# 23 instead of 24 tiles a group in a fused transformer-like kernel, seven steps of the recurrence beside each sorted unit, long operations moved between steps

## What is computed

```python
xn = layernorm(x)
x = x + linear_attention(xn) + moe0(xn)      # moe0: 16 experts of 176 units, top 6, softmax weights
xn = layernorm(x)
x = x + recurrence(xn) + moe1(xn)

def recurrence(x):                           # 512 numbers of state for each of the 4 sequences
    u = x @ W_in.T + b_in
    state = tanh(u[:, t] + state * gamma + beta)     # for t in 0 .. 511, one after the other
    return states @ W_out.T + b_out

def moe1(x):                                 # 8 experts of 176 units, top 2, and 2 shared experts
    topk_w, topk_idx = top_k(softmax(x @ gate.T), 2); topk_w /= topk_w.sum()
    y = sum over the 2 chosen e of topk_w * (silu(x @ wg[e].T) * (x @ wu[e].T)) @ wd[e].T
    return y + silu(x @ sg.T) * (x @ su.T) @ sd.T
```

## Time and profile before

| | us |
|---|---|
| median of 3 runs | 677.58 |
| lowest, highest | 676.92, 679.07 |
| the profiled execution | 680.39 |
| its span, first to last instruction | 678.80 |

### The profile page before, as it was taken

The page is one execution under the profiler, slowest core; times in us unless marked ns, Lnnn a source line. Parts: engine busy times, 40 slices in busy tenths (PEclk is TensorE's granted clock), DMA queues, the critical chain, the costliest instruction groups (busy, mean ns, idle before and its releaser), DMA issues. The chain is left out here.

```text
span 678.8 us, 12642 instructions
## 1 busy us (share of the span) xinstructions
PE 624.3 (92%) x3607; PEld 343.8 (51%) x3607; DVE 448.0 (66%) x1519; ACT 369.1 (54%) x1008; POOL 247.4 (36%) x267
## 2 busy tenths in 40 slices
PE   6999899999999988999999989999877899888985
PEld 2665344544444434444454434454554576656754
DVE  7873876567943767674677775567682756774666
ACT  2445445456446456567556666746456647563550
POOL 5246222222242125532225523223610342653483
PEclk8999999999999999999999999999987899988998
DMA  8103577773495435852556620507322455752133
GB/s 305 60 1 132 188 247 242 246 233 95 141 341 188 153 104 173 267 185 96 177 187 209 218 93 1 214 11 123 87 38 63 93 143 129 174 153 77 40 113 99
DMA packets 91228, 99.06 MB, mean 146 GB/s; under 512 B 30478, under 2 KB 81774, under 8 KB 90734
## 3 DMA queue, kind: packets, MB, share of 16 engines
q10 hardware_dynamic: 45840, 46.40, 20.9%
q1 hardware_dynamic: 39950, 37.21, 19.0%
q0 software_dynamic: 5376, 14.69, 7.2%
...
## 5 line engine op out<-in xcount | busy, mean ns | idle before, releaser
L1876 POOL TENSOR_TENSOR hl<-scr,hh 128x512 f16<-128x512 f32 (+2 forms) x100 | 115.9, 1159 | 288.7 <-ACT hh L1265 287.1
L1295 ACT ACTIVATE RING<-zbuf 128x16 f32<-128x16 f32 x512 | 111.0, 217 | 149.6 <-DVE zbuf L1732 145.3
L714 PE MATMUL G<-xT,W 128*128 128x512 f16 (+2 forms) x600 | 146.3, 380 | 4.9 <-ACT scr L1257 2.9
L714 PE MATMUL U<-xT,W 128*128 128x512 f16 (+2 forms) x600 | 147.2, 382 | 2.7 <-DVE scr L1747 2.7
L1732 DVE TENSOR_TENSOR_SCAN zbuf<-C,RING 128x32 f32<-128x32 f32 x350 | 77.0, 220 | 76.1 <-ACT RING L1295 75.7
L714 PE MATMUL Y<-hh,W 128*128 128x512 f16 x352 | 119.3, 380 | 6.7 <-POOL hl L1876 6.6
L714 PEld LDWEIGHTS U<-xT,W 128*128 128x128 f16 (+3 forms) x600 | 61.4, 103 | 72.4 <-DVE scr L1747 4.0
L714 PEld LDWEIGHTS G<-xT,W 128*128 128x128 f16 (+3 forms) x600 | 60.1, 102 | 69.7 <-issue 5.1
L1753 DVE TENSOR_TENSOR U<-U,CS 128x512 f32<-128x512 f32 x88 | 60.4, 686 | 39.2 <-PE U L714 32.7
L1257 ACT ACTIVATE scr<-G 128x512 f32<-128x512 f32 (+2 forms) x100 | 58.8, 588 | 47.1 <-PE G L714 46.6
L1265 ACT ACTIVATE hh<-scr 128x512 f16<-128x512 f32 (+2 forms) x100 | 61.8, 618 | 28.8 <-DVE scr L1747 26.1
...
...
## 6 DMA issues: line engine op xcount, KB each, us to landing
...
W<-parked SPq DMA_DIRECT2D x1, 3520.0 KB, 11.6
```

The source lines that it names most:

```text
L714: last = nc.tensor.matmul(bank_, w(wp), act(ap), start=start and n == 0, stop=stop and n == count - 1)
L1295: nc.scalar.activation(RING[:, (t + 1) % RING_T, ::2], zbuf[:, 1::2], ACT.Tanh).then_inc(state_done, 1)
L1876: nc.gpsimd.tensor_tensor(hl[rows, a, :], h32[a][rows, :], hh[rows, a, :], ALU.subtract)\
```

## The change

There are 23 tiles in a group. Two groups have 46 tiles, 23 tile units; the twelfth (pair 11) has the last tile of the first group and the first of the second. So there are 35 units: 0 to 2 shared, 3 to 25 tiles, 26 to 34 shared. A tile unit carries seven steps, a shared one six: 312 + 18 + 23 x 7 + 18 = 509 steps lie before unit 29, which has the last three. In a tile unit the seventh step follows step 5 on both engines. What was listed for units 26 and later stands one unit earlier, `hold_gamma` (a copy of gamma into PSUM for the scans of the last units) two.

A new table `UNIT_GAPS` names operations that are called behind step i of unit u instead of in front of a unit: the row copy of block 3, the exponential, the four input copies, and all heads and tails of the states of blocks 1 to 3. Those of block 1 move from the fronts of units 6 to 9 to units 1 to 4, those of block 2 from units 21 to 24 to units 20 to 23, those of block 3 from units 34 and 35 to units 30 to 33. The two turn buffers in PSUM (`HT`) change places.

```diff
+UNIT_STEPS = {"S": SLOTTED, "R": SLOTTED + 1}
-TILES = 24
+TILES = 23
...
-         + [("R", group, q) for group in (0, 1) for q in range(TILES // 2)]
+         + [("R", 2 * r // TILES, r) for r in range(len(GROUPS) * TILES // 2)]
...
-        HT = (G, C)
+        HT = (C, G)
...
-        UNITS_HELD = (0, 1, 2, 30, 31, 32, 33)
+        UNITS_HELD = (0, 1, 2, 28, 29)
...
-            5: [("shared_add", (0, Y[0])), ("norm_turn", (7, Y[1])), ("rows", (3, 0))],
-            6: [("logits", (7, Y[1][1])), ("rows", (3, 1)), ("split_states", (1, 0))],
-            7: [("inputs", (3, 0, Y[1])), ("exp", (7,)), ("split_states", (1, 1))],
-            8: [("inputs", (3, 2, Y[1])), ("split_states", (1, 2))],
-            9: [("rank", (3, Y[1][1])), ("split_states", (1, 3))],
-            10: [("scatter", (3, 0)), ("scatter", (3, 1))],
+            5: [("shared_add", (0, Y[0])), ("norm_turn", (7, Y[1]))],
+            6: [("logits", (7, Y[1][1]))],
+            7: [("inputs", (3, 0, Y[1]))],
+            8: [("inputs", (3, 2, Y[1]))],
+            9: [("rank", (3, Y[1][1]))],
+            10: [("more_inputs", (4,)), ("scatter", (3, 0)), ("scatter", (3, 1))],
...
-            21: [("split_states", (2, 0))],
-            22: [("split_states", (2, 1))],
-            23: [("split_states", (2, 2))],
-            24: [("split_states", (2, 3))],
-            26: [("attend", (2, Y[1]))],
-            30: [("hold_gamma", (BLOCKS,))],
-            32: [("shared_add", (1, Y[1]))],
-            34: [("split_states", (3, 0)), ("split_states", (3, 1))],
-            35: [("split_states", (3, 2)), ("split_states", (3, 3))],
+            25: [("attend", (2, Y[1]))],
+            28: [("hold_gamma", (BLOCKS,))],
+            31: [("shared_add", (1, Y[1]))],
...
+        UNIT_GAPS = {(5, 3): ("rows", (3, 0)), (5, 5): ("rows", (3, 1)),
+                     (7, 0): ("input_copy", (3, 0, Y[1][0])), (7, 2): ("input_copy", (3, 1, Y[1][1])), (6, 4): ("exp", (7,)),
+                     (8, 0): ("input_copy", (3, 2, Y[1][0])), (8, 2): ("input_copy", (3, 3, Y[1][1])),
+                     **{(1 + c, 3): ("states_head", (1, c)) for c in range(KH)},
+                     **{(1 + c, 5): ("states_tail", (1, c)) for c in range(KH)},
+                     **{(20 + c, 3): ("states_head", (2, c)) for c in range(KH)},
+                     **{(20 + c, 5): ("states_tail", (2, c)) for c in range(KH)},
+                     **{(30 + c, 2): ("states_head", (3, c)) for c in range(KH)},
+                     **{(30 + c, 4): ("states_tail", (3, c)) for c in range(KH)}}
...
+        def unit_gap(u, gap, share):
+
+            name, args = UNIT_GAPS.get((u, gap), (None, ()))
+            if name in share:
+                share[name](*args)
...
+        def steps_to(u):
+
+            return STEPS * TICKS0 + sum(UNIT_STEPS[UNITS[m][0]] for m in range(u))
+
+        def group_of_pair(r):
+
+            return (2 * r + 1) // TILES
...
             def unit_step(u, i):
-                step(TICKS0, SLOTTED * u + i)
+                state_at(steps_to(u) + i)
+                unit_gap(u, i, gaps)
...
-                unit_step(u, 5)
+                for i in range(5, UNIT_STEPS[kind(n)]):
+                    unit_step(u, i)
...
                 def unit_step(i):
-                    step(TICKS0, SLOTTED * u + i, u in UNITS_HELD)
-                    if u in UNIT_WOVEN:
+                    scan_at(steps_to(u) + i, u in UNITS_HELD)
+                    if u in UNIT_WOVEN and i < SLOTTED:
...
+                    unit_gap(u, i, {"states_tail": split_states})
```

78 lines of the change are left out of this document (44 added, 34 removed).

## The result

The changed kernel takes 673.53 us (median of 8 runs) beside 679.21 us for the kernel before (median of 8). The ratio is 0.992, 95% interval 0.9901 to 0.9939: faster by 5.4 us, give or take 1.3. The prediction was 672.0 us, 5.6 us saved. The profiled execution took 674.63 us with a span of 673.0 us; that of before 680.39 and 678.8. The forecast of 672.0 was counted from 677.58 us, the median of three runs; over eight the kernel before has 679.21. One of the eight runs of the changed kernel took 807.01 us at a granted clock of 0.75 and is left out of the ratio; the other seven took 671.8 to 675.9 us.

The account below looks back on a forecast made before the run. It took the scan-tanh chain on VectorE and ScalarE, held by operations between steps, as the bound where TensorE isn't full; -2.6 + 0 + 0.6 - 2.9 - 0.7 = -5.6 us off 677.58 gave 672.0 us, range 667 to 679.

Parts of the forecast that it names:

- Units 1 to 8: Units 1 to 8: 17.7 us of front stops removed, less seventh steps, gap operations and late input products; -2.6 us.
- The moves alone: Units 1 to 8: moving stages from fronts into gaps, without the 3.1 us for six seventh steps.
- Units 9 to 13: Units 9 to 13: seventh steps vanish in waits for the stores' DMA and the attention products; 0, bound +2.5 us.
- 14 to 18: Units 14 to 18: five units of 3.84 us, 19.2 us instead of 18.6; +0.6 us.
- rival (b): Units 9 to 18: the seventh step isn't absorbed, ten cost 5.1 us instead of 0.6; 676.5 us, no change; chance 0.20.
- Units 19 to 25: Units 19 to 26, afterwards 19 to 25: one tile unit goes and most of it is kept; -2.9 us.
- gap prices: Units 20 to 23: added to the 3.84 us chain, combines 0.6, head with silu 0.8, tail 0.6; 5.8 us each.
- the two units behind them: Two units behind units 20 to 23: 608.85 to 621.74 us as before; one seventh step hidden, the other costs 0.5 us.
- rival (a): Units 1 to 8 and 20 to 23: spread waits keep TensorE's clock low; 14.6 us in all, 682 at two thirds; chance 0.13.
- The shared units: Units 26 to 34: the recurrence ends in unit 29 instead of 33, freeing the last head before the gathers; -0.7 us.
- Behind the gathers: From the first of the last 16 GpSimd gathers to the end: number unchanged, so 36.4 us stays.
- The exponential: Gap of unit 6: exponential and table load cost 1.1 us; the skill page's draining would add 1.4 us, giving 673.3 us.

Follow-up runs that it names:

- e2_gaps24: Kernel before (24 tiles, six steps a unit) with only operations moved into gaps, block 3's heads and tails staying in front: 675.92 us, ratio 0.9958.
- e3_six: Changed kernel with six steps in a tile unit instead of seven, 23 tiles and gaps kept: 670.13 us, ratio 0.9868 to before.
- e6_pairs: e3_six with block 2's state head of one quarter and tail of the previous paired in one gap of units 19 to 23: 666.37 us, ratio 0.9795.
- e1_fronts: Changed kernel (23 tiles, seven steps) with every gap stage called in front of a unit again: 677.84 us, ratio 0.9982 to before.
- e12_filler24: Kernel before with nine more matmuls on zeros in front of unit 27, the first shared one: 676.98 us, ratio 0.9964.
- e11_hold_sooner: Kernel before with gamma copied into PSUM in front of unit 29 instead of 30, unit 29's scans reading it there: 678.82 us, ratio 0.9998.
- e4_filler: Changed kernel with seven more matmuls on zeros in each of units 20 to 24: 672.71 us, ratio 0.9922 to before.
- e5_late_states: e3_six with block 1's heads and tails in gaps of units 8 to 11 instead of 1 to 4: 668.07 us, ratio 0.9830 to before.
- e7_both: e3_six with the edits of e5_late_states and e6_pairs, and block 0's combines one unit later: 663.10 us, ratio 0.9760 to before.
- e8_filler: e7_both with nine more matmuls on zeros in front of the first shared unit behind the tiles: 664.26 us, ratio 0.9763 to before.
- e9_pairs_both: e7_both with block 1's heads and tails paired too, in gaps of units 7 to 11: 659.62 us, ratio 0.9723 to before.
- e10_changed_again: Changed kernel run again without any edit: 674.06 us, ratio 0.9915 to before.

## Why the prediction was right, and where it wasn't

**Units 1 to 8 (-2.6 predicted, -3.3 measured).** By the means of three executions each it is -2.5 us. The mechanism is the predicted one: the long stops go, shorter ones come. Its terms were less exact than their sum. The moves alone were -2.6 - 3.1 = -5.7 us in it; the executions of six steps with gaps (e2_gaps24, e3_six, e6_pairs: 50.5 to 50.8 us) give -4.6. Units 1 to 4 were too cheap: 2.4 for four tails and 2.0 for four heads, 4.4 us, against 6.3 measured. The tails of units 1 and 2 meet GpSimd's, which I hadn't looked for, and in unit 3 VectorE has no room left (6.99 of 7.6 us busy). The rest of the moves brought 9.6 to 11.4 us where I had 10.1. The seventh step was taken at its full 0.51 us six times, 3.1 us; the executions with gaps give 2.2 in the mean, 1.5 to 3.0 by single pairs, and those with fronts (e1_fronts) 0.2 to 1.0. So the moves brought about 1 us less than forecast, the seventh steps cost about 1 us less, and the two errors cancel.

**Units 9 to 13 (0, +0.2), 14 to 18 (+0.6, +0.5).** Right, and for the reasons given: e3_six has the same 25.4 us in units 9 to 13 without the seventh steps, and units 14 to 18 come at 3.83 to 3.84 us each, the chain's length. So rival (b), which had all ten steps paid, has its refutation in one row of the table.

**Units 19 to 25 (-2.9, -0.5).** A clear miss. Units 20 to 23 are 5.86 to 5.88 us long for 5.8 predicted, so the gap prices were right (0.90, 0.57 and 0.58 us for 0.8, 0.6 and 0.6). Unit 19 is 0.7 us longer than the 4.4 predicted, since one combine there waits 0.74 us for its gather's DMA. The failed step is "the two units behind them take 608.85 to 621.74": I took unit 25's 8.98 us over unchanged as unit 24's. It takes 10.5, because TensorE's clock falls in front of it. I had this mechanism as rival (a), but priced it through all of units 20 to 23, where the chain hides it, and dismissed it with the clock of 0.94 in units 20 to 24 of before. That is a mean over 30.5 us which hides a fall at its end, to 0.85 and 0.79 in units 23 and 24 of before. Here it bites in the unit where no chain hides it, since TensorE's attention products follow directly. The two filler kernels show it and its price at this place and in front of the first shared unit, 2.2 and 1.7 us.

**The shared units (-0.7, -2.9).** The failed step is the same one in reverse: I kept the 1.97 us wait of the earlier trace rows and didn't see that the passes behind it ran at the lower level (1.87 us for the first, 2.77 for the second, against 1.46 at the full clock), so that a kernel in which the clock doesn't fall there is 1.7 us faster (e12_filler24). Of that the changed kernel shows 1.1 net, as unit 26 takes 6.01 and not 5.43 us. The other 1.8 us lie between the next unit and the first gather, and the traces split them by unit:

- 0.74 us: unit 27 takes 4.46 us, unit 28 of before 5.20. This is the other side of the 0.58 us by which unit 26 is longer. The last combine lies in the first shared unit now (1.03 us at 623.51), so the chain comes to the next unit later, when its products are further on. The two units together take 10.47 us, and 10.63 in e12_filler24, which has the clock up and no combine there; TensorE's first passes of the three shared units stand 4.35 and 3.91 us apart in both.
- 0.95 us: unit 28 takes 3.41 us, unit 29 of before 4.36. That is the earlier hold of gamma: e11_hold_sooner has 3.42 us there with nothing else changed. I had costed it at nothing. In e11_hold_sooner only 0.5 us of it reach the first gather; why more does in the changed kernel is open.
- 0.12 us: from the next first scan to the gather (3.86 against 3.98 us).

The recurrence's earlier end, from which I had argued my 0.7, gives little of it: the stretch from the second shared unit to the first gather is 11.7 to 11.9 us long in e1_fronts, e4_filler and the changed kernel, where it ends in unit 29, and just as long in e3_six, e5_late_states and e6_pairs, where it ends in unit 33. In e7_both, e8_filler and e9_pairs_both it is 12.6 us, because their last combine lies in that second unit (5.20 us); in the kernels with 24 tiles it is 13.5 (13.1 in e11_hold_sooner).

**Behind the gathers** the end comes 36.8 us after the first, 0.4 later than the 36.4 taken as fixed. e11_hold_sooner shows the same 36.8 with its earlier first gather, so what the hold brings is given back there; in e2_gaps24 and e12_filler24, without it, it is 36.3.

**The total** was right because these errors cancel: +2.4 us in units 19 to 25, -2.2 in the shared units. In both the clock is the largest part; it falls in front of unit 24 in the changed kernel and in front of the first shared unit in the kernel before, in e1_fronts at both places and in e7_both at neither. So that the total came within 0.2 us is luck; that units 1 to 8 and 14 to 18 came as forecast is not. One of its alarms was set too coarsely: it called itself wrong if the granted clock of units 1 to 8 were under 0.8. It is 0.87 over the whole stretch (0.89 before), but 0.76, 0.79, 0.71 and 0.68 in units 3, 4, 5 and 6. In unit 3 VectorE decides; in unit 6 rival (a) is at work: TensorE is busy throughout, and unit 6 takes 5.38, 5.69 and 6.64 us in three executions of the same code, for 5.0 predicted. ScalarE's second silu in unit 6 of e10_changed_again waits for its products:

```profile
514.33 0.32 ACT L1299 ACTIVATE scr<-U 128x176 f32<-128x176 f32 x1 [1.06 <-PE U L1067]
```

**The exponential.** In the changed kernel the tanh ends the gap of unit 6 as early as the load and the exponential allow: load at 515.01, 1.28 us, exponential at 516.31, tanh at 516.44. The scans around it stand 1.50 us apart, 1.0 more than a step. The Trainium skill (ScalarE: Activation LUTs, What ACT_TABLE_LOAD costs) gives a further 1.38 us of draining for every switch of tables; no run here shows it, neither at this switch nor at the one back in unit 7 (load at 519.30, silu at 520.60).
